# Edge MLP of a four-layer graph network: attribute product for tile pairs, in float32r passes of 256 columns

## The reference, cut to what matters

```python
def mish(x):
    return x * jnp.tanh(jax.nn.softplus(x))
edge_feat = jnp.concatenate([x[src], x[dst], edge_attr], axis=-1)
h = mish(edge_feat @ W1 + b1)
messages = mish(h @ W2 + b2)
agg = jax.ops.segment_sum(messages, dst, num_segments=x.shape[0])
```

## Time and profile before

| | us |
|---|---|
| median of three timed runs (1145.32 to 1147.47) | 1146.72 |
| the profiled execution, its own time | 1148.59 |
| its span, first to last instruction | 1146.8 |
| TensorE busy | 1061.8 |
| VectorE busy | 840.4 |
| ScalarE busy | 562.7 |
| GpSimd busy | 563.9 |
| from 600 to 640 us of the span, inside the edge MLP: TensorE busy | 39.86 of 40 |
| VectorE, ScalarE, GpSimd there | 32.35, 31.44, 27.38 of 40 |

### The profile page before, as it was taken

How to read it: one execution, slowest core, us unless ns; L and a number is a source line. 1 busy time by engine, 2 the same in 40 slices (tenths; PEclk the granted TensorE clock), 3 DMA queues, 4 the chain that set the end, 5 groups by cost and what they waited for, 6 DMA issues and landing times. The chain is left out here.

```text
span 1146.8 us, 15596 instructions
## 1 busy us (share of the span) xinstructions
PE 1061.8 (93%) x4389; PEld 601.8 (52%) x4421; DVE 840.4 (73%) x1901; ACT 562.7 (49%) x986; POOL 563.9 (49%) x518
## 2 busy tenths in 40 slices
PE   3979887889989997999999999999999999999997
PEld 1543232265565544656555655565556556446664
DVE  5996878857373154778887888788878867849997
ACT  0222332430312222577777777777777734116664
POOL 1981213225423331868876666666666200027774
PEclk9989999999999998999999999999999999999999
DMA  8997997574031015875555545555444020036765
GB/s 304 358 407 302 342 402 243 191 253 150 26 122 44 15 41 189 191 214 111 111 106 97 100 94 98 97 100 93 99 97 73 1 77 1 9 103 196 209 204 169
DMA packets 60326, 173.19 MB, mean 151 GB/s; under 512 B 12661, under 2 KB 13205, under 8 KB 52696
## 3 DMA queue, kind: packets, MB, share of 16 engines
q0 software_dynamic: 31536, 72.01, 27.9%
q1 hardware_dynamic: 28712, 100.19, 23.5%
HBM read 160.18 MB, written 11.98 MB: 150 GB/s over the span
## 5 line engine op out<-in xcount | busy, mean ns | idle before, releaser
L1791 PE MATMUL PS<-wide,hidT 128*128 128x512 f32 x672 | 302.1, 592 | 2.3 <-DVE hidT L1667 0.5
L751 POOL DMA_INDIRECT rec_scratch<-rec_src,slot_row x84 | 103.1, 1227 | 233.9 <-DMA rec_scratch<-rec_src,slot_row 218.3
L1791 PEld LDWEIGHTS PS<-wide,hidT 128*128 128x128 f32 x672 | 128.8, 192 | 122.7 <-issue 120.4
L1725 ACT ACTIVATE wide<-PS 128x512 f32<-128x512 f32 x168 | 100.3, 597 | 100.7 <-PE PS L1775 64.2
L1609 POOL DMA_INDIRECT pair_sum<-table_j,counts_rec x84 | 136.5, 1625 | 26.8 <-issue 25.3
L1928 POOL DMA_INDIRECT u_space<-table_j,wide x87 | 86.0, 988 | 110.5 <-DMA table_j<-agg_space 83.6
L1601 POOL DMA_INDIRECT pair_sum<-table_i,counts_rec x84 | 89.5, 1065 | 95.7 <-PE PS L1775 59.7
L1730 ACT ACTIVATE wide<-wide,two 128x512 f32<-128x512 f32 x168 | 120.8, 719 | 6.1 <-DVE wide L1660 6.0
L1660 DVE SCALAR_TENSOR_TENSOR wide<-wide 128x512 f32<-128x512 f32 x168 | 116.4, 693 | 5.8
L1735 ACT ACTIVATE wide<-wide 128x512 f32<-128x512 f32 x168 | 105.8, 630 | 5.3
L1618 POOL DMA_INDIRECT rec_scratch<-rec_src,slot_row x84 | 87.9, 1047 | 40.5 <-issue 21.6
(11 more groups left out here) (348 smaller groups left out, 1882.9 us busy)
## 6 DMA issues: line engine op xcount, KB each, us to landing
pieces<-basis_rows SPq DMA_DIRECT2D x56, 1024.0 KB, 7.9
ring<-basis_low SPq DMA_DIRECT2D x30, 256.0 KB, 6.9
w_scratch<-pieces SPq DMA_DIRECT2D x112, 32.0 KB
counts_rec<-rec_scratch SPq DMA_DIRECT2D x1, 2856.0 KB, 9.7
rec_scratch<-rec_src,slot_row POOLq DMA_INDIRECT x168, 2.4
rows_in<-in_rows_in SPq DMA_DIRECT2D x2, 1024.0 KB, 14.1
w_rel<-w_scratch SPq DMA_DIRECT2D x1, 2048.0 KB
w_rel<-L_gnn_W SPq DMA_DIRECT2D x2, 1024.0 KB, 7.0
```

The lines of the kernel that those rows point to most:

```text
L751: nc.gpsimd.indirect_dma_start(out=rec3_dram, out_offset=bass.IndirectOffsetOnAxis(ap=slot_row[:, 1, t:t + 1], axis=0), in_=rec, in_offset ...
L1725: nc.scalar.activation(grow[l][:, t % 2, :], PS[:, bank, :], ACT.Exp).then_inc(sem(f"exp{l}"), 1)
L1791: m = nc.tensor.matmul(o, hidT[:, t % 2, k * P:(k + 1) * P], w2[:, k, :], start=False, stop=(k == KT - 1), skip_group_check=True)
```

## The change

The stage now works in pairs of tiles. `half_pre(h)` takes the place of `pre(t)`: of the pair that h belongs to, it makes the first 256 hidden columns (h even) or the last 256 (h odd), for both tiles. It transposes two blocks of each tile into the bank, and adds the attribute product of each block of hidden columns over 256 edges at once. That product is float32r, one pass each: `attr` has the rounded attributes on partitions 0 to 63 and the remainder on 64 to 127, the weights are doubled on both halves, and there are two sets, `w_attr_hi` and `w_attr_lo`. `hidT` has four halves in place of two tiles. All loops run one step further ahead: TensorE's step s is `message(s-1)`, `half_pre(s+2)`, `seg_sum(s-2)`, and s starts at -2.

Turned groups lie on 64 partitions; ScalarE rounds every one (`high_turn`) and VectorE makes every remainder (`keep_turn`). Twelve go ahead of the loop. The bias split stands behind them. GpSimd has eight buffers and is two tiles ahead in place of three.

```diff
-            GOT3, LAG3, LATE5, HOT3, TURN_GROUP = 9, 3, 8, 5, 4
-            attr = sb("attr", [P, ET * P], F32, p3)
-            w_attr = sb("w_attr", [P, D], F32, p3)
+            GOT3, LAG3, LATE5, HOT3, TURN_GROUP = 8, 2, 8, 5, 4
+            attr = sb("attr", [P, ET * P], F32R, p3)
+            w_attr_hi = sb("w_attr_hi", [P, D], F32R, p3)
+            w_attr_lo = nc.alloc_sbuf_tensor_at("w_attr_lo", [P, D], F32R, offset=counts_at + 4 * ET * REC)
...
-            TURNS_ACT, TURNS_AHEAD = 10, 16
-            TURNS_AFTER = {-1: range(16, 19), 0: range(19, N_TURN)}
+            TURNS_AHEAD = 12
+            TURNS_AFTER = {-2: range(12, 14), -1: range(14, 17), 0: range(17, 19), 1: range(19, N_TURN)}
...
-                sp.dma_start(w_attr[0:ED, :], a["L2_gnn_W1"][2 * D:2 * D + ED, :]).then_inc(sem("w_attr_in"), 16)
+                for half in range(2):
+                    sp.dma_start(w_in[half * ED:(half + 1) * ED, :], a["L2_gnn_W1"][2 * D:2 * D + ED, :]).then_inc(sem("w_attr_in"), 16)
...
-                        pool.wait_ge(sem("pre_mm"), t - GOT3 + 1)
+                        pool.wait_ge(sem("pre_mm"), (t - GOT3) // 2 * 2 + 2)
...
+                keep_turn(0)
+                dve.wait_ge(sem("w_attr_hi"), 1)
+                nc.vector.tensor_tensor(w_attr_lo[:], w_in, w_attr_hi[:].bitcast(F32), ALU.subtract).then_inc(sem("w_attr_lo"), 1)
+                for j in range(1, TURNS_AHEAD):
                     keep_turn(j)
+                split_bias()
+                for s in range(-2, ET + 1):
...
-                for k in range(KT):
-                    m = nc.tensor.matmul(PS[:, pre_bank(t), k * P:(k + 1) * P], w_attr[:, k * P:(k + 1) * P],
-                                         attr[:, t * P:(t + 1) * P], start=False, stop=True, skip_group_check=True)
+                def half_pre(h):
+                    first = h // 2 * 2
+                    if h % 2 == 0:
+                        for t in (first, first + 1):
+                            pe.wait_ge(sem(f"pair3_{t % GOT3}"), 16 * (t // GOT3) + 16)
...
+                    for k in range(2):
+                        for q in range(2):
+                            c = (h % 2 * 2 + k) * P
+                            nc.tensor.matmul(at[:, k, q, :], pair_sum[:, (first + q) % GOT3, c:c + P], ident[:],
+                                             is_transpose=True, start=(k == 0 and q == 0), stop=False, skip_group_check=True)
+                    for k in range(2):
+                        c = (h % 2 * 2 + k) * P
+                        for w in (w_attr_hi, w_attr_lo):
+                            m = nc.tensor.matmul(PS[:, half_bank(h), 2 * k * P:2 * (k + 1) * P], w[:, c:c + P],
+                                                 attr[:, first * P:(first + 2) * P], start=False, stop=(w is w_attr_lo), skip_group_check=True)
+                    m.then_inc(sem("pre_mm"), 1)
+
+                def bias(t):
+                    pe.wait_ge(sem("mish0"), min(t + 2, ET))
```

More of the change, by code:

```diff
@@ L1623, in _ @@
                 gather_i(1)
+                gather_i(2)
                 add_j(0)
-                gather_i(2)
                 add_j(1)
                 gather_i(3)
-                for t in range(1, ET):
+                add_j(2)
+                gather_i(4)
+                add_j(3)
+                gather_i(5)
+                for t in range(4, ET):
                     if t + LAG3 < ET:
                         gather_i(t + LAG3)
-                    if t >= 2:
-                        add_j(t)
+                    add_j(t)
                     if t >= LATE5:
@@ L1643, in _, with split_bias @@
                 nc.vector.memset(ones[:], 1.0).then_inc(sem("b2_ones"), 1)
-                nc.vector.memset(w_attr[ED:P, :], 0.0).then_inc(sem("w_attr_zero"), 1)
                 nc.vector.memset(none, 0.0).then_inc(sem("none"), 1)
[L1646 to L1652, removed]
+                def split_bias():
+                    dve.wait_ge(sem("b2_in"), 16)
+                    for j in range(3):
+                        if j:
+                            dve.wait_ge(sem("b2_split"), 2 * j)
+                        nc.vector.tensor_copy(b2_part[j], b2_in).then_inc(sem("b2_split"), 1)
+                        dve.wait_ge(sem("b2_split"), 2 * j + 1)
+                        nc.vector.tensor_tensor(b2_in, b2_in, b2_part[j], ALU.subtract).then_inc(sem("b2_split"), 1)
                 def grown(l, t):
@@ L1741, in high_part, with high_turn @@
                     nc.scalar.copy(mes_hi[:, t % KEPT3, :], mes[:, t % 2, :]).then_inc(sem("mes_hi"), 1)
-                for j in range(TURNS_ACT):
+                def high_turn(j):
                     act.wait_ge(sem("attr_tp"), j + 1)
-                    nc.scalar.copy(attr[:, j * D:(j + 1) * D], PS[:, j % NT, :]).then_inc(sem("attr_T"), 1)
-                for s in range(-1, ET + 1):
+                    nc.scalar.copy(attr[0:ED, j * D:(j + 1) * D], PS[0:ED, j % NT, :]).then_inc(sem("attr_hi"), 1)
+                high_turn(0)
+                act.wait_ge(sem("w_attr_in"), 32)
+                nc.scalar.copy(w_attr_hi[:], w_in).then_inc(sem("w_attr_hi"), 1)
+                for j in range(1, TURNS_AHEAD):
+                    high_turn(j)
+                for s in range(-2, ET + 1):
                     if 0 <= s - 1 < ET:
                         grow_exp(1, s - 1, mes_bank(s - 1))
-                    if 0 <= s + 1 < ET:
-                        grow_exp(0, s + 1, pre_bank(s + 1))
+                    if 0 <= s + 2 < ET:
+                        grow_exp(0, s + 2, half_bank(s + 2))
+                    for j in TURNS_AFTER.get(s, ()):
+                        high_turn(j)
                     if 0 <= s - 1 < ET:
@@ L1790, in message @@
                     for k in range(KT):
-                        m = nc.tensor.matmul(o, hidT[:, t % 2, k * P:(k + 1) * P], w2[:, k, :], start=False,
+                        c = (k % 2 * 2 + t % 2) * P
+                        m = nc.tensor.matmul(o, hidT[:, t // 2 % 2, k // 2, c:c + P], w2[:, k, :], start=False,
                                              stop=(k == KT - 1), skip_group_check=True)
@@ L1843, in _ @@
                     turn(j)
-                pe.wait_ge(sem("w_attr_in"), 16)
-                pe.wait_ge(sem("w_attr_zero"), 1)
-                for s in range(-1, ET + 2):
+                pe.wait_ge(sem("w_attr_hi"), 1)
+                pe.wait_ge(sem("w_attr_lo"), 1)
+                for s in range(-2, ET + 2):
                     if s == 2:
                         clear()
-                    if s == 0:
+                    if s == 1:
                         pe.wait_ge(sem("b2_ones"), 1)
```

79 lines of the change are left out of this document (36 added, 43 removed).

## The result

| | before | changed |
|---|---|---|
| timed executions | 12 | 12 |
| median, us | 1147.0 | 1156.68 |
| lowest and highest, us | 1142.07, 1149.96 | 1152.16, 1168.5 |
| profiled execution: own time, span | 1148.6, 1146.8 | 1152.16, 1150.2 |

The changed kernel is slower: ratio 1.010, 95% interval 1.0072 to 1.0127, or +9.7 us. The forecast had the sign (+3.7 us) and the wide range of 1137 to 1157 holds the time, but the own range of the forecast (1147 to 1154) doesn't, and the size is out: +9.7 against +3.7 us. Note two things. The changed kernel's executions spread over 16 us, the old one's over 8. And the profiled execution is the fastest of its twelve: its span is only 3.4 us longer. So the trace first explains a difference of 3.4 us, and a part of the 9.7 isn't in it.

What follows compares the result with a forecast made beforehand. TensorE's own work bounds the edge MLP before (5.46 us a tile), a two-step loop through the segment sum after (5.40). Start +9.0, steps -4.8, end -0.5 make +3.7 us: 1150.4 us; own range 1147 to 1154, wide 1137 to 1157.

Steps and rivals of the forecast that it cites:

- Attribute product: TensorE, edge MLP: eight passes (0.81 us) become four float32r matmuls (0.45 us), cutting its work from 5.46 to 5.10 us.
- the float32r rival: The new attribute matmuls miss full rate: 1158 us at 0.21 us each, 1228 at 0.43; chance 0.05.
- Loop (c): Two-step cycle: message, exponential, VectorE to `mes_lo`, segment sum, message t+2; 10.81 us for two tiles, 5.40 a tile.
- The rival in which it doesn't bind: The sum's wait is absorbed, so VectorE and ScalarE bind at 5.23 us a tile: 1137 us; chance 0.15.
- Steps: Edge MLP: 80 steps, each 0.06 us shorter, give -4.8 us; the last step but one, without layer-0 work, -0.5.
- The start: Stage start: paired order and VectorE's longer queue make `w2` of message 2 9.0 us late, bounds 6 to 12.
- the rival on the clock: TensorE, idle in pieces at the start, runs `w2` of message 0 at 1.2 GHz: 1154 us; chance 0.15.
- the gathers: GpSimd's gathers with eight buffers in place of nine: costed at nothing, as its data lie about three steps ahead.

Runs made afterwards that it cites:

- late: Changed kernel with the segment sum of message t-2 issued between the fourth and fifth pass of message t; 1141.66 us, ratio to before 0.9946.
- before_late: Kernel before with only the segment sum of message t-2 moved into the middle of a message; 1144.94 us, ratio to before 0.998.
- only_hi: Changed kernel without the attribute weights' low part, two of four short matmuls of each message left out; 1154.0 us, ratio to before 1.0075.
- again2: Changed kernel, unaltered, one more execution; 1154.33 us.
- again: Changed kernel, unaltered, run once more; 1158.29 us, ratio to before 1.0087.
- again3: Changed kernel, unaltered, on the chip used for hold; 1156.44 us, twelve executions.
- shift: Changed kernel with GpSimd's buffer wait and stage-5 scatter put ahead of the gather, so gathers start about 1.3 us later against the clamps; 1155.24 us.
- hold: Changed kernel with every second gather on GpSimd held until ScalarE has ended a message's exponential; 1152.68 us, ratio to before 1.0046.
- start: Changed kernel with VectorE's bias split first, weight roundings after five turned groups, 16 groups ahead of the loop; 1145.77 us, ratio to before 0.9991.
- both: Changed kernel with the moved segment sum and the reordered stage start together; 1126.0 us, ratio to before 0.9812.

## Why the prediction was right and wrong

**Attribute product: right.** The first matmul starts 0.20 us ahead of the second and the others 0.12 apart, where 0.11 was forecast; the float32r rival falls. TensorE's work of 5.10 us a tile shows in both as 5.13.

**Loop (c) binds: right.** It was worked out as 10.81 us for two tiles and measured as 10.75. The distance from `mes_lo` to the sum is 0.51 (0.53 forecast). The rival in which it doesn't bind falls by late, before_late and only_hi: opening it gives 16 us, shortening TensorE's queue gives nothing. Steps: forecast -4.8 and -0.5 us, measured 438.44 - 445.65 = -7.2 in an execution of the short period (-6.8 in the 80 steps, -0.4 at the last tile).

**The start: mis-sized.** Forecast +9.0 us, measured 39.70 - 27.65 = +12.05. Its parts, against the forecast starts of `w2` of messages 0, 1 and 2 (474.2, 483.5, 488.6):

- Message 0 at 475.77, 1.6 late. The second half of the weights was issued at 453.0 and ScalarE's copy started at 456.88, where 455.6 was taken from the single load of the earlier trace rows; this 1.3 us went through all twelve turned groups.
- Message 1 at 485.74, another 0.6. TensorE had idled 2.7 us, and the last clears and the bias took longer at the lower clock.
- Message 2 at 491.87, another 1.1, by the 4.69 us of message 1. So the rival on the clock came in part, in this trace not in message 0 but in the clears and message 1. I looked for an idle piece long enough ahead of message 0, and not in the wait for the last two groups. In again2 and only_hi it came in message 0 too: its eight passes took 5.29 us there. again2's start is no longer for it (39.66 us); its message 1 took 3.60 us.

Start, steps and rest make +12.05 - 7.2 - 1.6 = +3.2 us, and the stage began 0.2 later: the +3.4 of the two traces. The rest has nothing of the change in it and varies between 218.0 and 221.5 over all runs. Without it, the change costs +4.9 in an execution of the short period, against a forecast of +3.7.

**The step that failed: that a step has one length.** The prediction took VectorE's and ScalarE's part of loop (c), 5.23 us, from one step of the trace of before and used it for all, and it costed the gathers at nothing. In that trace the part is the same in every step: TensorE's full queue sets the pace, 5.46 us, and GpSimd's first gather starts 0.4 us ahead of a clamp in 54 of 70 cases and lengthens it in none (2 slow clamps in all, both beside the adding gather). With TensorE's queue no longer full, the four traces of the changed kernel show two ways to run. In the short one (the first trace and again2) the gathers meet the clamps where these aren't lengthened; every second gather takes 1.50 us, which costs nothing, since GpSimd has time. In the long one (again and again3) the clamps are lengthened: 0.35 us more on VectorE in every second tile, of which 0.29 reach the loop that binds (11.04 in place of 10.75 us for two tiles), 11.4 us over the stage. In again3 half of the executions run in each, and the first twelve fall into six up to 1155.1 and six from 1158.3 on, without a clean gap. If half of them were long ones, the median would hold some 5 of these 11.4 us. That is an estimate; 4.9 + 5 comes near the 9.7 measured. I had costed GpSimd's edits at nothing, because its data lie three steps ahead. That was true of its data, as shift shows; it left out that its instructions, by when they run, can slow VectorE's.

So two terms were wrong: the start, 3 us too small, and GpSimd's gathers, at nothing in place of some 5 us of the median.

The Trainium skill (SBUF — State Buffer, "Who interferes with whom") says that VectorE in certain modes and GpSimd share one port pair by a lock, that whoever issues first gets it and that the other is blocked. No trace here shows the port or the mode. That the two lengthen each other fits. That the order of issue decides does not: in each of these cases the gather was issued first, or at the same time.

| gather ahead of the clamp by, us | clamp, us | gather, us | seen |
|---|---|---|---|
| 0.0 to 0.1 | 0.43 | 1.0 | changed, 34 times |
| 0.4 | 0.43 | 1.08 | before, 54 |
| 0.4 | 0.42 | 1.3 | late, 27 |
| 0.5 to 0.6 | 0.42 | 1.3 | hold, 35 |
| 0.65 | 0.57 to 0.59 | 1.0 | late, 33 |
| 0.75 | 0.42 | 1.5 | changed, 33 |
| 0.9 | 0.58 to 0.65 | 1.25 | again, 33 |

Which of the two is lengthened goes with how far the gather had got, but in no simple order; other VectorE instructions overlap the gather as well (`mes_lo` in late and again). The traces don't show a block for a whole instruction either. In again the gather ran from 598.75 to 600.00, by a profile whose spans on GpSimd are rough, and the clamp that came due at 599.62 was through at 600.24, 0.19 us late.

**What stays open.** What decides which way an execution runs: shift didn't change it, start seems to, and neither was made to tell. What inside a gather makes a clamp wait at 0.65 and 0.9 us and not at 0.5 or 0.75. How much of late's 5.9 us against both are its slow clamps. And both was seen in five executions and one trace, so a longer period of it may exist.

## What to carry to other kernels

When work is taken from the engine that bounds a loop, look for the cycle that closes over several steps and hold the next gain against it: here 0.36 us of TensorE's work were worth 0.08 a tile, until the segment sum that closed the cycle was moved; then 0.26 came (late), and 0.33 with the other start as well (both). Once the full queue that kept all engines in step is gone, an engine with time to spare can still slow the bound one, by when it runs; compare the spread of the timed runs, not the medians alone, and if it has grown, take a second trace before explaining the first. Holding the idle engine's instruction behind the critical one costs a line and made the short period the only one seen, in six executions.

## What the runs showed of the hardware

- A clamp of 128x512 float32 on VectorE, SBUF to SBUF, takes 0.43 us alone. Beside the issue of an indexed DMA on GpSimd it takes that, or up to 0.62 us, and the issue takes 1.0 to 1.5 us. Which of them is lengthened goes with the distance between the two starts and is not told by the order of issue alone (table above).
- Such a meeting locks in: from 500 to 920 us the first gather lengthened a clamp in every second tile (35 of some 38 in again), or nearly never (at most 8 slow clamps of any kind in the traces of the short period).
- TensorE idled for 2.7 us at the full granted clock and went back to work; within the next 1.2 us the clock fell to its lower level (1.2 GHz), until 487, and the eight passes that followed the clears took 4.69 us in place of 3.60.
- Four float32r matmuls with 256 columns, on changing weights, start 0.12 us apart, and the first of them 0.20 us ahead of the second.
- The register operations ahead of a matmul with an address from a register hold it 0.50 to 0.54 us behind the end of the instruction waited for, in 77 of 79 steps of the changed kernel's trace.
